# A four-layer graph network on one core: squares summed through transposes, and the scaled adjacency product made without transposes

## The reference, cut to what matters

```python
H = (adj != 0)                       # node x edge
w = adj.reshape(N, -1)[:, :C]        # weights of the edges, adj's first row
Dn = where(H @ w > 0, 1 / (H @ w), 0)
Be = 1 / H.sum(axis=1)
out = Dn[:, :, None] * (H @ (Be[:, :, None] * (H.T @ (x @ W.T)))) + b

h = relu(conv(x, adj, W1, b1))       # hidden width 512
h = layer_norm(h, gamma, beta)       # mean and variance over the 512
y = conv(h, adj, W2, b2)
x = layernorm(x + (y + x))           # layers 1 to 3 follow in the same manner
```

## Time and profile before

| | |
|---|---|
| Time, median of 3 runs | 1393.01 us (1392.85 to 1393.94) |
| The profiled execution | 1393.31 us, its span 1391.2 us |
| TensorE busy | 1376.9 us (99%) |
| TensorE weight loads | 1335.9 us (96%) |
| VectorE busy | 1134.6 us (82%) |
| ScalarE busy | 1122.7 us (81%) |
| GpSimd busy | 1003.6 us (72%) |
| Granted TensorE clock, mean | 0.997 |

### The profile page before, as it was taken

The page is one execution under the profiler, slowest core; times in us unless marked ns, Lnnn a source line. Parts: engine busy times, 40 slices in busy tenths (PEclk is TensorE's granted clock), DMA queues, the critical chain, the costliest instruction groups (busy, mean ns, idle before and its releaser), DMA issues.

```text
span 1391.2 us, 35333 instructions
## 1 busy us (share of the span) xinstructions
PE 1376.9 (99%) x10946; PEld 1335.9 (96%) x10946; DVE 1134.6 (82%) x4092; ACT 1122.7 (81%) x2639; POOL 1003.6 (72%) x1059
## 2 busy tenths in 40 slices
PE   8999999999999999999999999999999999999997
PEld 8999999999999999999999999999999999999996
DVE  7888788888887887788888878878888888888896
ACT  6777887887888878878878888888788788887776
POOL 5758778778778787787787787777877877877531
PEclk9999999999999999999999999999999999999999
DMA  4100110110100101101101101011011011010000
GB/s 143 36 20 20 40 39 20 39 40 20 39 29 31 39 21 39 39 20 40 39 20 40 32 28 39 21 39 39 21 39 39 20 40 37 23 40 21 8 22 34
DMA packets 29961, 47.17 MB, mean 34 GB/s; under 512 B 3408, under 2 KB 12240, under 8 KB 29776
## 3 DMA queue, kind: packets, MB, share of 16 engines
q1 hardware_dynamic: 29776, 44.91, 10.1%
HBM read 28.12 MB, written 16.78 MB: 32 GB/s over the span
## 4 chain that ended last, share of the span: by engine, by line
PE 98%; ACT 1%; issue 0%; DVE 0%; DMA 0%; SPq 0%; ACTq 0%; DVEq 0%
PE psum L374 95%; PE psum L473 2%; PE psum L417 1%; DMA n_s<-w2T_in 0%; ACT x L1010 0%; ACT tk L1172 0%; ACT h_hi L991 0%; DVE w2c_lo L1785 0%; DVE w2g L1767 0%; ACT w2c_hi L991 0%; ACT r_f L1015 0%; SPq L291 0%; ACT h_f L1015 0%; DVE n_st L1575 0%; DVE n_s L260 0%
## 5 line engine op out<-in xcount | busy, mean ns | idle before, releaser
L208 POOL TENSOR_TENSOR h_lo<-h_f,h_hi 128x512 fp32r<-128x512 f32 x120 | 154.9, 1291 | 93.6 <-ACT h_hi L991 93.4
L1010 ACT ACTIVATE x<-n_s,n_shift,n_rstd 128x256 f32<-128x256 f32 x384 | 208.0, 590 | 4.2 <-DVE n_shift L1599 4.1
L215 POOL TENSOR_TENSOR r_lo<-r_f,r_hi 128x512 fp32r<-128x512 f32 x123 | 158.7, 1292 | 44.1 <-ACT r_hi L991 43.9
L2229 POOL TENSOR_TENSOR n_s<-tk,mask 128x512 f32<-128x512 f32 x60 | 62.5, 1041 | 154.1 <-DVE mask L1652 133.0
L1575 DVE BATCH_NORM_STATS2 n_st<-n_s 128x6 f32<-128x256 f32 x384 | 141.9, 412 | 2.2
L374 PE MATMUL psum<-v_hi,h_hi 128*128 128x256 f32 x512 | 137.8, 292 | 2.0 <-ACT h_hi L991 2.0
L374 PE MATMUL psum<-A_f,x 128*128 128x128 f32 x1024 | 135.5, 275 | 0.6 <-ACT x L1010 0.5
L1015 ACT ACTIVATE h_f<-psum,columns 128x256 f32<-128x256 f32 x256 | 107.6, 472 | 34.8 <-PE psum L374 34.7
L374 PE MATMUL psum<-v_lo,h_hi 128*128 128x256 f32 x512 | 133.3, 282 | 0.0
L374 PE MATMUL psum<-gx_hi,w1T_hi 128*128 128x256 f32 x512 | 132.3, 281 | 0.0
L374 PE MATMUL psum<-gx_hi,w1T_lo 128*128 128x256 f32 x512 | 131.9, 281 | 0.0
(11 more groups left out here) (173 smaller groups left out, 5200.1 us busy)
## 6 DMA issues: line engine op xcount, KB each, us to landing
x_in<-x_in_dram SPq DMA_DIRECT2D x64, 256.0 KB, 2.8
out<-x SPq DMA_DIRECT2D x64, 256.0 KB, 2.0
at_in<-adjT SPq DMA_DIRECT2D x64, 128.0 KB, 2.2
x<-v_in SPq DMA_DIRECT2D x3, 256.0 KB, 5.7
n_s<-w2T_in SPq DMA_DIRECT2D x2, 256.0 KB, 3.3
r_f<-w1T_in SPq DMA_DIRECT2D x2, 256.0 KB, 5.1
h_f<-wab_in SPq DMA_DIRECT2D x2, 256.0 KB, 5.6
rows<-rows_in SPq DMA_DIRECT2D x1, 256.0 KB, 6.0
```

Of the source, the lines that this page charges most:

```text
L208: return e.tensor_tensor(dst[1][:], src, f(dst[0][:]), ALU.subtract).then_inc(signal, 1)
L215: e.tensor_tensor(r_s[1][:, half], r_f[:, half], f(r_s[0][:, half]), ALU.subtract).then_inc(r_lo[h], 1)
L1010: last = act.activation(dst[:, g, :], nm.s[:, g, :], ACT.Identity, scale=nm.rstd[:, g:g + 1], bias=nm.shift[:, g:g + 1])
L2229: pool.tensor_tensor(n4.s[:], tk[:], bc(mask[:], [C, 2, D], 2), ALU.mult).then_inc(tk_masked, 1)
```

## The change

1. `squares(p)`, for pairs 0 to 60: instead of two matmuls with a column of ones, two transposes of sq1 into columns 384 to 511 of P's banks, and VectorE adds up the 128 columns of each (`add_columns`, a new first step of `wide_var`) into `h_sq`.
2. In the loop (n = 7 to 61), `Tr` is gone from TensorE and `copy_GT` from ScalarE. Because the matrix is symmetric before its rows are scaled, its transpose is the same matrix with its columns scaled. VectorE makes `dinv` early in its body (`invert_degrees`), SyncE writes it to a DRAM row and reads it back spread over all partitions into `dinv_b` (`spread_dinv`), VectorE adds the high and low halves into Gd without scaling (`add_halves`), and GpSimd multiplies Gd by `dinv_b` into GT (`scale_GT`). `round_GT` reads GT from SBUF instead of PSUM.
3. Some semaphores that were raised once by several steps are put together; this changes no order.

The squares on TensorE, in the function and in the loop:

```diff
         def squares(p):
             pe.wait_ge(sq_sum, upto(p))
+            if p + 1 < LAST:
...
+                for g in range(2):
+                    last = pe.transpose(psum[:, bank("P", p) + g, 3 * C:4 * C], sq1[:, g, :], ident[:])
+                last.then_inc(pe_did["P"], 1)
+                return
...
                 squares(n - 1)
-                pe.wait_ge(ax2_lo, n - 2)
-                Tr(n)
                 AXB(n - 2)
```

SyncE's new step, which stands between `reload(n + 2)` and `store(n - 5)`:

```diff
+            def spread_dinv(p):
+                sp.wait_ge(dinv_made, upto(p))
...
+                sp.dma_start(dinv_row, dinv[:]).then_inc(dinv_stored, 16)
+                sp.wait_ge(dinv_stored, spread(p))
...
+                sp.dma_start(dinv_b[:], dinv_row.partition_broadcast(C)).then_inc(dinv_spread, 16)
```

VectorE's new steps (`invert_degrees` is the first part of the old `scale_G`, with one reduce for each graph in the loop):

```diff
+            def add_halves(p):
...
+                dve.tensor_reduce(Gd[:], psum[:, b[0]:b[1] + 1:2, 0:2 * C].rearrange("p g (h c) -> p g c h", h=2),
+                                  AX_X, ALU.add).then_inc(gd_made, 1)
...
+            def add_columns(p):
+                b = bank("P", p)
+                dve.wait_ge(pe_did["P"], upto(p))
+                dve.wait_ge(hm2, upto(p))
...
+                dve.tensor_reduce(h_sq[:], psum[:, b:b + 2, 3 * C:4 * C], AX_X, ALU.add).then_inc(sq_added, 1)
```

GpSimd's new step, and its place in the loop:

```diff
+            def scale_GT(p):
+                pool.wait_ge(gd_made, upto(p))
+                pool.wait_ge(dinv_spread, spread(p))
...
+                pool.tensor_tensor(GT[p % 2][:], Gd[:], dinv_b[:].rearrange("p c g -> p g c"), ALU.mult).then_inc(gt_made, 1)
...
                 low_h1(pool, n - 3)
+                scale_GT(n)
                 if n + 1 < NP:
                     split_weights(n + 1)
                     spread_high(n + 1)
                     spread_low(n + 1)
+                low_GT(n)
                 make_xb(pool, n - 1)
-                low_GT(n)
                 low_p(pool, n - 1)
```

ScalarE's loop:

```diff
                 square_mean(n - 1)
-                copy_GT(n)
+                round_GT(n)
                 root_h(n - 1)
-                round_GT(n)
                 make_x3(n - 4)
```

More of the change, by code:

```diff
@@ L90, in build @@
         Gl, Gd = sb("Gl", [2, C]), sb("Gd", [2, C])
+        dinv_row = nc.dram_tensor("dinv_row", (C, 2), F32, kind="Internal").ap()
+        dinv_b = sb("dinv_b", [C, 2])
         GT = [sb(f"GT{b}", [2, C]) for b in range(2)]
@@ L95, in build @@
         sq, sq2, sq1 = sb("sq", [KH, 2, C]), sb("sq2", [2, 2, C]), sb("sq1", [2, C])
-        h_mean2 = sb("h_mean2", [2])
+        h_mean2, h_sq = sb("h_mean2", [2]), sb("h_sq", [2])
         h_veps, h_std, h_rstd = sb("h_veps", [2]), sb("h_std", [2]), sb("h_rstd", [2])
@@ L192, in bank, with in_loop, spread, turned @@
             return BANK_OF.get((stage, pair), BANK[stage])
+        def in_loop(pair, lag):
+            return FIRST <= pair + lag < LAST
+        def spread(pair):
+            return 16 * (pair - FIRST + 1)
+        def turned(pair):
+            return pair + 1 if pair < FIRST else FIRST + max(0, pair - LAST + 1)
         def inputs(p):
@@ L359, in body @@
                     reload(n + 2)
+                if n < LAST:
+                    spread_dinv(n)
                 store(n - 5)
@@ L1063, in round_GT @@
                     act.wait_ge(pe_did["GP"], upto(p - 2))
+                if in_loop(p, 0):
+                    act.wait_ge(gt_made, upto(p))
+                    copy(GT_s[p % 2][0][:], GT[p % 2][:]).then_inc(gt_hi, 1)
+                    return
                 copy(GT_s[p % 2][0][:].rearrange("p a b -> p (a b)"),
@@ L1202, in round_w2 @@
             def round_w2():
-                act.wait_ge(w2_centred, 1)
-                copy(w2c_s[0][:, :, 0:D], w2g[:]).then_inc(w2c_hi, 1)
+                act.wait_ge(w2_step, 2)
+                copy(w2c_s[0][:, :, 0:D], w2g[:]).then_inc(w2_step, 1)
             def fill():
@@ L1667, in scale_G @@
-                dve.wait_ge(dn_3, upto(p))
+                if in_loop(p, 0):
+                    for g in range(2):
+                        last = dve.tensor_reduce(dn[:, g:g + 1], psum[:, b[g], 2 * C:2 * C + 2], AX_X, ALU.add)
+                else:
+                    last = dve.tensor_reduce(dn, psum[:, both, 2 * C:2 * C + 2], AX_X, ALU.add)
+                last.then_inc(dn_step, 1)
+                dve.wait_ge(dn_step, 3 * p + 1)
+                dve.tensor_scalar(dn_max[:], dn, TINY, None, ALU.max).then_inc(dn_step, 1)
@@ new lines, in invert_degrees @@
+                dve.wait_ge(dn_step, 3 * p + 2)
+                dve.reciprocal(dn_inv[:], dn_max[:]).then_inc(dn_step, 1)
+                dve.wait_ge(dn_step, 3 * p + 3)
+                if p > FIRST and in_loop(p - 1, 0):
+                    dve.wait_ge(dinv_stored, spread(p - 1))
+                dve.scalar_tensor_tensor(out=dinv[:], in0=dn, scalar=0.0, in1=dn_inv[:],
+                                         op0=ALU.is_gt, op1=ALU.mult).then_inc(dinv_made, 1)
+            def add_halves(p):
+                b = bank("G", p)
+                if in_loop(p - 1, 0):
+                    dve.wait_ge(gt_made, upto(p - 1))
+                else:
+                    dve.wait_ge(pe_did["Tr"], turned(p - 1))
+                dve.tensor_reduce(Gd[:], psum[:, b[0]:b[1] + 1:2, 0:2 * C].rearrange("p g (h c) -> p g c h", h=2),
+                                  AX_X, ALU.add).then_inc(gd_made, 1)
@@ L1693, in invert_edges @@
                 dve.reciprocal(be_inv[:], be[:]).then_inc(be_made, 1)
+            def add_columns(p):
+                b = bank("P", p)
+                dve.wait_ge(pe_did["P"], upto(p))
+                dve.wait_ge(hm2, upto(p))
+                if begun(p - 1):
+                    dve.wait_ge(hv, upto(p - 1))
+                dve.tensor_reduce(h_sq[:], psum[:, b:b + 2, 3 * C:4 * C], AX_X, ALU.add).then_inc(sq_added, 1)
             def wide_var(p):
                 b = bank("P", p)
+                if p + 1 < LAST:
+                    add_columns(p)
+                    dve.wait_ge(sq_added, upto(p))
                 h_var = psum[:, b:b + 2, D + 4]
                 dve.wait_ge(hm2, upto(p))
-                dve.scalar_tensor_tensor(out=h_var, in0=psum[:, b:b + 2, D + 2], scalar=1.0 / DH,
+                dve.scalar_tensor_tensor(out=h_var, in0=h_sq[:] if p + 1 < LAST else psum[:, b:b + 2, D + 2],
+                                         scalar=1.0 / DH,
                                          in1=h_mean2[:], op0=ALU.mult, op1=ALU.subtract).then_inc(hv, 1)
@@ L1988, in body @@
                 count_nonzero(n - 5)
+                invert_degrees(n)
                 low_x1T(n - 2)
@@ L1991, in body @@
                 low_ax2(n - 3)
-                scale_G(n)
+                add_halves(n)
                 if n + 1 < NP:
```

74 lines of the change are left out of this document (44 added, 30 removed).

## The result

The changed kernel took 1419.7 us (median of 4 runs, 1418.5 to 1420.1) against 1393.0 (4 runs, 1392.9 to 1393.9): a ratio of 1.0189, 95% interval 1.0171 to 1.0206. It is slower by 26.7 us. The forecast was 1384.0.

The account below looks back on a forecast made before the run. TensorE, 99% busy at 21.21 us a body, was the bound; its 0.36 saving shrank to 0.16 waiting for p_lo. 55 x 0.16 = 8.8, plus 0.5 ahead of the loop, took 1393.3 to 1384.0; range 1372 to 1394.

Parts of the forecast that it names:

- TensorE's own work: TensorE per loop body: two transposes replace the squares' matmuls and Gd transposes, saving 0.36 us, 21.21 to 20.85.
- (b) h_sq: VectorE's added reduce of 2 x 128 PSUM values, 0.42 us: variance starts 0.44 later, x1 0.30 later.
- (e): ScalarE loses a 0.4 us copy and has room; round_GT waiting for scale_GT costs nothing up to some 0.6 us.
- long ring: Two-body chain from n_s over variance, ScalarE, GpSimd's stream, p_lo and GP back to n_s: 42.11 us, 21.05 per body.
- the short one over x1: One-body chain from VectorE's n_s to x1, its TensorE transposes and back to n_s: 20.9 us, doing little harm.
- The fill: Ahead of the loop, the six squares of pairs 0 to 5 save up to 1.1 us; 0.5 counted.
- (a): VectorE's degree steps move into 1.23 us idle ahead of x1T_lo; 1.1 us freed, lost waiting at n_s: no net effect.
- (c): SyncE's two dinv transfers, each 2.0 to 3 us, end at 614.2 to 616.2, before scale_GT at about 619.
- The cover: Time to spare between dinv's transfers landing and GpSimd's scale_GT needing them: 3 us.
- (d): GpSimd's added scale_GT: 0.74 us busy, 0.70 of its stream, 0.11 coming back; p_lo 0.59 later from GpSimd alone.
- The rival on the slower side: Expensive scale_GT on GpSimd ahead of p_lo, or late dinv_b, makes the kernel slower: 1400.5 at the upper bound; 14%.

Follow-up runs that it names:

- x3 first: Changed kernel with ScalarE's make_x3 moved ahead of root_h, nothing else: 1401.1 us (1.0053).
- unused reduce: Changed kernel with squares summed by the old matmul, plus a same-shaped VectorE reduce ahead of the variance whose result nobody uses: 1409.5 us (1.0113).
- squares alone: Kernel before with only the squares' transposes, add_columns and h_sq; Gd still transposed on TensorE: 1479.6 us (1.0616).
- way to GT alone: Changed kernel with squares done as before (matmul with a column of ones, no h_sq): 1385.5 us (0.9941).
- changed, sums in PSUM: Changed kernel with the reduced squares written to PSUM instead of SBUF: 1406.2 us (1.0091).
- squares alone, sums in PSUM: Kernel before with only the squares' transposes and reduce, the reduced squares written to PSUM instead of SBUF: 1417.7 us (1.0172).

## Why the prediction was wrong

*TensorE's own work* was right: 0.39 us a body saved where I had 0.36 (0.14 for Tr, 0.22 to 0.25 for the squares).

*(b) h_sq* was right in size, 0.42 and 0.46, and wrong in reach. It had the variance start 0.44 later, and from there p_f, p_hi, the sum for layer 2, gx_lo, the n1 statistics and x1: I followed what uses the variance, and not what only stands behind it. *(e) ScalarE "has room"* is the step that failed. It has room on average (79% busy), but root_h stops its list until h_veps is there, x3 stands next, and x3 ended only the hand-over of 0.06 us ahead of Ax3. I read ScalarE at the places that my rings passed through, and x3 was at none of them. The long ring over p_lo and the short one over x1 were both worked out; the ring n_s, variance, root_h, x3, Ax3 was the one that bound, at 21.37 to 21.8 us where the long ring was forecast at 21.05. In the changed kernel TensorE waits for p_lo once, for 0.3 us, so no run measures the long ring as forecast. One premise of it did not hold: p_lo stands behind xb now, but in 30 bodies it still waits for p_hi, which is late with the variance (14.4 us in all). The run with x3 first and the run with the unused reduce show it from two sides.

*A cost that was missing*: the variance step with both operands in SBUF, 0.21 us a body on average (21.00 less 9.4, by 55), 13.5 us in the end. I gave the step no new price because its shape was unchanged. In the kernel with the squares alone the same omission is worth 62 us.

*A gain that was missing*: GT_hi out of the way of x3, 0.23 us a body. Without it the change would probably have been slower still.

The ring can be read step by step from the start of n_s to the start of the next body's. Each number is the mean over 35 bodies of a run's trace, in us:

| step | before | way to GT alone | unused reduce | changed, sums in PSUM | changed | squares alone, sums in PSUM | squares alone |
|---|---|---|---|---|---|---|---|
| n_s to the variance step | 3.45 | 3.46 | 3.96 | 3.90 | 3.89 | 3.92 | 3.91 |
| variance step to h_veps | 0.20 | 0.20 | 0.20 | 0.20 | 0.41 | 0.20 | 1.31 |
| h_veps to h_std | 0.19 | 0.19 | 0.19 | 0.19 | 0.19 | 0.19 | 0.19 |
| h_std to x3 | 0.38 | 0.16 | 0.16 | 0.16 | 0.16 | 0.38 | 0.38 |
| x3 to Ax3's weight load | 1.14 | 1.20 | 1.14 | 1.14 | 1.14 | 1.13 | 1.13 |
| Ax3's weight load to the next n_s | 15.86 | 15.86 | 15.79 | 15.82 | 15.80 | 15.79 | 15.79 |
| body | 21.23 | 21.08 | 21.45 | 21.41 | 21.61 | 21.61 | 22.70 |

In the first two columns TensorE has no gap; in the others it waits for x3, and the last step falls to about 15.79. So the ring had some 0.07 us of room before, an estimate from 15.86 less 15.79. A body of the changed kernel against the kernel before: 0.44 (reduce) + 0.21 (operand) - 0.22 (GT_hi) - 0.06 (the room) = 0.37; its measured body is 0.38 longer, 20.8 us in 55 bodies. Of the other 6 us the trace has 4.1 ahead of the loop and 1.7 behind it.

*The fill*: I expected up to 1.1 us gained and counted half. The five intervals between the first six transposes of x1 took 88.8 us instead of 85.5, 3.3 more, and the first of them came 0.8 later. With the way to GT alone they took 85.5, so the squares' edit causes this. The unused reduce alone makes them 87.2, and with the sums in PSUM instead of SBUF the changed kernel takes 87.7: the reduce and the operand cost time there too.

*(a)* was right that the moved steps cost nothing in the end, but it did not see HT grow by 0.95 us.

*(c)* The transfers landed in 3.0 and 4.2 us, where 2 to 3 was given to each:

```profile
dinv_b<-dinv_row SPq DMA_DIRECT2D x55, 128.0 KB, 4.2
dinv_row<-dinv SPq DMA_DIRECT2D x55, 1.0 KB, 3.0
```

The cover held: in the body at 604 dinv_b was issued at 604.55, so it landed at about 608.8, and scale_GT ran at 610.46. 1.7 us to spare, not 3.

*(d)* scale_GT was right:

```profile
610.46 0.75 POOL L2291 TENSOR_TENSOR GT<-Gd,dinv_b 128x256 f32<-128x256 f32 x1
```

0.75 and 0.71 to the next, where GT_lo takes 0.73: the operand with a step of 8 bytes costs nothing extra here. That agrees with the rule of the Trainium skill (GPSIMD Engine Reference, Performance pitfalls for Q7 kernels), which charges only steps of over 8 bytes. *The rival on the slower side* named GpSimd's multiply as its mechanism, and was wrong in that: the loss came over VectorE and ScalarE.

**The version to keep** is the way to GT alone: 1385.5 us, 0.6% under the kernel before, and below every version with the squares' transposes.

## What to carry to other kernels

Where TensorE is 99% busy, look for the rings that are level with it: at each of its stages, how long before the stage did its input end? What had next to nothing to spare here was an input that had nothing to do with the edit, except that it stood in an in-order list behind an instruction that had. When a step is made later, list what is queued behind each instruction that waits for it, on every engine, before following the data. And a new operand's place counts as much as its size.

## What the runs showed of the hardware

- A VectorE instruction of 128 x 2 values with both inputs in SBUF took 0.17 us alone, 0.63 beside a GpSimd multiply of 0.61, and 1.29 beside one of 1.30; both times it ended within 0.03 us of GpSimd's. With starts that the profile can't tell apart it also took 0.17, and then GpSimd's multiply took 0.64. With one input in PSUM it took 0.17 in all 64 cases.
- VectorE's `tensor_scalar` on 256 fp32 values from SBUF to SBUF took 0.28 in the kernel before, where it began 0.02 us after a GpSimd instruction that then took 0.89 instead of the 0.74 that it takes elsewhere, and 1.23 to 1.3 where a long GpSimd instruction was running. No run gives it another operand, so the cause is not tested. The same comparison with an accumulator, 128 values at a time, took 0.28 each in all 128 cases, beside GpSimd's squares too. The next step there, a `tensor_scalar` of 128 x 2 values, then waited in its place: 0.65 instead of 0.17, from 613.96 to 614.61, where GpSimd's instruction ended at 614.59.
- Two transposes of 128x128 took 0.14 us of TensorE's queue in the changed kernel and 0.17 in the kernel before, two fp32 matmuls with a single column 0.36.
- A store of 1 KB from 128 partitions, 8 bytes each, to a DRAM row landed in 3.0 us, and the read of that row back to all partitions in 4.2.
